# Layer two's attention on VectorE: clip and multiply half by half

## The reference

```python
Q, K = _l2norm(heads(Wq)), _l2norm(heads(Wk))
cos_sim = jnp.clip(jnp.einsum('bhtd,bhsd->bhts', Q, K), -0.999, 0.999)
scores = 1.0 - jnp.arccos(cos_sim) / jnp.pi
W = jnp.power(jnp.maximum(scores, EPS), 16.0)
W = W / (jnp.sum(W, axis=-1, keepdims=True) + EPS)
out = jnp.einsum('bhts,bhsd->bhtd', W, V)
```

## Time and profile before

| | |
|---|---|
| median of 3 runs | 6949.82 us (6949.76 to 6949.85) |
| the profiled execution | 6951.07 us, span 6949.3 us |
| mean granted TensorE clock | 0.709 of full speed |
| instructions of lines 1209 and 1214 | 1024 each |

### The profile page before, as it was taken

The page is one execution under the profiler, slowest core; times in us unless marked ns, Lnnn a source line. Parts: engine busy times, 40 slices in busy tenths (PEclk is TensorE's granted clock), DMA queues, the critical chain, the costliest instruction groups (busy, mean ns, idle before and its releaser), DMA issues. The chain is left out here.

```text
span 6949.3 us, 55640 instructions
## 1 busy us (share of the span) xinstructions
PE 3988.7 (57%) x17072; PEld 1356.5 (20%) x17072; DVE 6639.4 (96%) x6316; ACT 6429.0 (93%) x3748; POOL 3429.4 (49%) x1422
## 2 busy tenths in 40 slices
PE   5777767777677776454454454454454444454555
PEld 3222222222222242011111111121111111111112
DVE  7899999999999967999999999999999999999997
ACT  3699999999999934999999999999999999999997
POOL 0244444444444400656556565565656556565654
PEclk8888888898988887565666556565665665566557
DMA  3100000000000032000000000000000000000003
GB/s 130 56 14 14 16 12 16 12 16 11 16 11 16 7 138 85 6 15 8 9 15 9 8 15 9 8 15 9 11 12 9 8 15 9 8 15 9 15 6 99
DMA packets 238999, 157.45 MB, mean 23 GB/s; under 512 B 148998, under 2 KB 222617, under 8 KB 237418
## 3 DMA queue, kind: packets, MB, share of 16 engines
q1 hardware_dynamic: 238826, 155.32, 8.0%
HBM read 95.74 MB, written 59.51 MB: 22 GB/s over the span
## 5 line engine op out<-in xcount | busy, mean ns | idle before, releaser
L1306 POOL TENSOR_TENSOR work<-work 128x1776 f32<-128x1776 f32 (+3 forms) x696 | 2149.0, 3088 | 55.3
L1098 PE MATMUL psS<-q_stack,k_stack 96*128 96x512 bf16 x2048 | 1034.6, 608 | 1757.4 <-DVE work L1214 1691.5
L750 POOL TENSOR_SCALAR work<-work 128x2048 f32<-128x2048 f32 x512 | 970.6, 1896 | 1218.8 <-DVE work L952 1199.4
L940 DVE SCALAR_TENSOR_TENSOR work<-work,psS 128x1024 f32<-128x1024 f32 x1024 | 1217.2, 1213 | 44.7 <-ACT work L899 44.5
L1303 POOL TENSOR_SCALAR work<-work 128x1776 f32<-128x1776 f32 (+2 forms) x174 | 290.8, 1671 | 1953.2 <-ACT work L1188 1945.9
L1209 DVE TENSOR_SCALAR work<-psS 128x1024 f32<-128x1024 f32 x1024 | 1204.7, 1218 | 41.5 <-PE psS L1098 17.2
L1214 DVE TENSOR_TENSOR work<-psS,work 128x1024 f32<-128x1024 f32 x1024 | 1200.3, 1213 | 0.0
L899 ACT ACTIVATE work<-psS 128x1024 f32<-128x1024 f32 x1024 | 1152.2, 1125 | 50.1 <-PE psS L768 49.5
L1220 DVE SCALAR_TENSOR_TENSOR work<-work 128x2048 f32<-128x2048 f32 x512 | 1139.0, 2283 | 30.1 <-ACT work L1184 30.1
L768 PE MATMUL psS<-q_stack,k_stack 102*128 102x512 bf16 x2048 | 709.8, 433 | 654.4 <-DVE work L940 620.5
L914 ACT ACTIVATE work<-work 128x2048 f32<-128x2048 f32 x512 | 1032.2, 2016 | 2.4 <-POOL work L750 2.4
(11 more groups left out here) (140 smaller groups left out, 3812.6 us busy)
## 6 DMA issues: line engine op xcount, KB each, us to landing
qk_parts<-work SPq DMA_DIRECT2D x64, 384.0 KB, 3.2
q_stack<-qk_parts SPq DMA_DIRECT2D x384, 64.0 KB, 2.3
k_stack<-qk_parts SPq DMA_DIRECT2D x384, 64.0 KB, 2.3
xT_store<-work SPq DMA_DIRECT2D x2, 4096.0 KB, 16.5
ffn_in<-xT_store SPq DMA_DIRECT2D x64, 128.0 KB, 2.5
work<-in_x SPq DMA_DIRECT2D x1, 4096.0 KB, 14.2
xn_store<-work SPq DMA_DIRECT2D x1, 4096.0 KB, 13.0
work<-xn_store SPq DMA_DIRECT2D x4, 1024.0 KB, 11.7
```

What stands on the lines that cost most here:

```text
L750: nc.gpsimd.tensor_scalar(slot, slot, F32_MAX, 0.0, ALU.min, ALU.max).then_inc(s_m, 1)
L940: nc.vector.scalar_tensor_tensor(part, part, 0.5 / SHEP_EPS, m.psS[half][:, :], ALU.add, ALU.mult).then_inc(s_y, 1)
L1098: last = nc.tensor.matmul(m.psS[half][:, q * 512:(q + 1) * 512], m.k_stack[b][0:ROWS, kt * P:(kt + 1) * P], m.q_stack[b][0:ROWS, c:c + 512 ...
L1306: nc.gpsimd.tensor_tensor(part, part, part, ALU.mult).then_inc(s_pp, 1)
```

## The change

VectorE does clip, product, clip, product in each unit instead of clip, clip, product, product: the second loop over the halves is merged into the first. Waits, signals, operands and the number of instructions are the same.

```diff
@@ clip_and_square
                     dve.wait_ge(s_qk, 2 * g + half + 1)
                     nc.vector.tensor_scalar(cosine(j, p)[:, 0, cols], m.psS[half][:, :], COS_MAX, -COS_MAX,
                                             ALU.min, ALU.max).then_inc(s_cl, 1)
-                for half in range(2):
-                    cols = slice(half * 1024, (half + 1) * 1024)
                     dve.wait_ge(s_cl, 2 * g + half + 1)
                     nc.vector.tensor_tensor(square(p)[:, 0, cols], m.psS[half][:, :], cosine(j, p)[:, 0, cols],
                                             ALU.mult).then_inc(s_q, 1)
```

## The result

The changed kernel takes 7015.73 us (median of 4 runs, 7015.07 to 7016.61) against 6949.84 for the kernel before: +65.9 us, a ratio of 1.0094 with a 95% interval of 1.0077 to 1.0112. The profiled execution took 7015.33 us, 64.3 more than that of before. The forecast was 7010, +60, with a range of 6985 to 7037.

The account below looks back on a forecast made before the run. VectorE was taken to set the pace, with ScalarE nearly full too. The terms +125 - 4 - 48 - 12 = +61, rounded to +60, gave a forecast median of 7010 us, range 6985 to 7037.

Parts of the forecast that it names:

- (a): VectorE, each product right behind its clip: waiting costs 0.122 us, 1024 times, +125 us; old clip-to-clip excess gone, -4.
- (b): VectorE's clips behind products: half 0's scores come earlier, so some 305 stalls of 0.155 us go, -48 us.
- (c): Last product to third tangent: with VectorE slower, ScalarE is on time in every batch without a ReLU, -12 us.
- (d): Line 1228: its 34 us waiting for GpSimd's last square go, but count nothing beyond (c), as ScalarE's path covers them.
- The rival that would have counted it in full: Line 1228, GpSimd's port: the gain counts in full, -34 in place of -12, about 6988; chance 0.11.
- half of 46: Product behind its clip: rival of a longer hand-over, gap 0.08 us, +46 us, 7056, chance 0.06; range takes in half.
- the marks named beforehand: Signs expected in the changed kernel's profile: idle times, unit spacing, line 1228's mean, and VectorE's and ScalarE's waits.
- The rival *faster: Product starts behind its clip at the pipelined 1.131 us, leaving only 52 us of stalls gained; 6920, chance 0.05.

Follow-up runs that it names:

- the control: The changed order with the product reading a constant tile but keeping its wait for the clip right in front; 7017.81 us, 64.3 over the kernel before.
- the two runs of 6945 and 6951: Kernel before with one score matmul less for half 0: 6945.33 us; kernel before with the first product of 329 units cut in two: 6951.44 us.
- the run with half the dose: The kernel before, its order kept, with the first product of each unit waiting for both clips; 7004.61 us, 51.1 over before.

## Why the prediction was right

Point by point, by its own steps.

(a) *The product behind its clip, +125.* Right in kind, and a little too small, by two errors of opposite sign. Clip to product is 1.248 us on average where 1.253 was worked out from the earlier trace rows, and the control shows that the wait makes it: 1024 x (1.248 - 1.131) = 119, not 125. The 1218 ns taken for a clip had the longer clips behind stalls in their mean; in the changed kernel a clip takes 1213. What the step had not seen is that the product itself takes 1224 ns in place of 1213 once it was waited for, and that the next instruction follows 1.141 behind instead of 1.131: another 11 us. Both together: the rows give 4.78 for a unit, 2.39 for each half, against twice 1.131: 1024 x (2.39 - 2.262) = 131, with the nanoseconds of all starts 130 us. The old 1.14 from clip to clip, counted at -4, was the same thing: it stood behind the clips that had stalled, 1.131 behind the others.

(b) *The stalls, -48.* Right for this change: line 1209's idle time went from 25.4 us to 1.8, and where a clip directly follows a product, in 332 places of the kernel before, the distance was 1.279 on average against 1.131, which makes 49 us. The reason was half of it. It is TensorE that is late, but the two halves share one stall, and where only the first half is made faster, half of the stall moves to the second clip (the two runs of 6945 and 6951). The changed order is free of that since it gives both halves two VectorE instructions.

(c) *ScalarE gives back 12.* Right: in the changed kernel every one of the 53 batches without a ReLU has its third tangent some 10.5 us behind the last product, and the sum of these distances falls from 570.2 to 556.9, by 13; ScalarE's lateness alone is worth 13.7 us in the kernel before and nothing in the changed one.

(d) *GpSimd's last square, nothing beyond (c).* Right: 3.8 us, not resolved from none, when it is taken away from the kernel before, and VectorE's wait for ScalarE rises by 29 us in its place. The rival that would have counted it in full is out.

The sum was +61. With what was found for each term it is 130 - 4 - 49 - 13 = 64, against 64.2 between the spans of the two traces and 65.9 between the medians. So the term that was mis-sized is (a), by 5 us, less 2 in (b) and (c). That the sum comes this close is partly luck: (a)'s two errors offset each other in part, and the runs of one kernel spread by 1.5 us. The range's upper end, 7037, lies 4 above what its own reason gives (7010 and half of 46); it decides nothing here.

Of the marks named beforehand: idle time before products, 36 forecast for the whole kernel and 34.5 found in the stretch; four instructions of a unit not closer than 4.77, 4.78 found; line 1228's mean near 480, 478; VectorE's wait at the tangents some 40, 42.6; ScalarE's waits for products up by 60, found up by 53.

The rival *faster*, the case of the rule in the Trainium skill ("VectorE: DVE Perf Modes", section "The DRAIN you can't avoid") that a semaphore between chained operations costs nothing, doesn't hold here: taking the wait out and leaving the order took 84 us off. Its own figure for the case without the cost, 6920, stood against a measured 19.3 under before, 6930.5 against the median of before. The reason was right in kind, since a part is taken back behind ScalarE, but it is 34 us, where the rival took 22.

## What to carry to other kernels

On VectorE, which is the bound here, two instructions of which the second waits for the first did not cost the same in either order: one independent instruction between them hid the signal. Here the wait cost 0.127 us, twice in each unit, against a stall of 0.15 us once in two units of three. Idle time in the groups showed only about a quarter of that cost; the distance between starts showed all of it. And time that is taken off one of two nearly full engines must be followed to the other: without the wait, shortening GpSimd's work was worth 2 us, and shortening ScalarE's then brought 49 more.

## What the runs showed of the hardware that was not expected

An instruction of VectorE that stood at a wait runs some 10 ns longer than one that came through without, and the next start is 10 ns later with it (1.141 in place of 1.131): the product's range is 1210 to 1217 ns in the kernel before and 1223 to 1227 in the changed one, from the views of one line, in before, after and the run with half the dose:

```profile
L1214 DVE TENSOR_TENSOR work<-psS,work x1024: 1210/1214/1217, 2714.6 to 6859.0; 128x1024 f32<-128x1024 f32 x171
```

```profile
L1212 DVE TENSOR_TENSOR work<-psS,work x1024: 1223/1224/1227, 2713.5 to 6921.8; 128x1024 f32<-128x1024 f32 x171
```

```profile
L1214 DVE TENSOR_TENSOR work<-psS,work x1024: 1214/1220/1226, 2714.2 to 6911.3; 128x1024 f32<-128x1024 f32 x171
```

(The three numbers behind the count are the shortest, the median and the longest, in ns.) In the run with half the dose both kinds stand in one kernel, 1214 to 1226. What it waited for made no difference: in the kernel before, the 370 clips that stood waiting, 312 of them behind a product and 55 behind the tangents, take 1224 to 1227 ns, as the one of 1.23 us in the earlier trace rows, and the other clips 1210 to 1223, with a median of 1214. Why, no run tells: it was seen with the ring and with the constant tile as the other operand.
